# A mixture-of-experts stage whose gate and up products change sides: weight chunks stationary, copied per tile by VectorE

## The chip, the cores and the metric

The kernel runs on one core of a Trainium2 chip. The metric is the device time of one execution in microseconds (us). The kernel before took 1597.97 us, the median of three runs that lie between 1597.82 and 1600.06 us.

## The reference, cut to what matters

The input is 16 x 256 = 4096 rows of 128 numbers. Six blocks follow each other, each on the layer-normalised rows and added back: a quantised feed-forward block, attention, the feed-forward block again, a mixture of experts (MoE), windowed attention, the MoE again. The MoE is the part that the change touches:

```python
logits = xf @ router_w.T                     # 8 experts, top 2 for each row
topk_scores = topk_scores / topk_scores.sum(-1, keepdims=True)
h = jax.nn.silu(xf @ wg) * (xf @ wu)         # per expert: 128 -> 512, twice
acc = acc + w[:, None] * (h @ wd)            # 512 -> 128
```

All of it is float32.

## The kernel before, in words

The rows stay in SBUF as 32 tiles of 128. Each block is a phase; at its end all engines meet (`ended`). In the MoE phase (class `Moe`) the logits and the routing come first. A row goes to two experts, so there are 8192 row copies, sorted by expert and padded to whole tiles of 128 that belong to one expert: `NS = 72` tiles in each of the two MoE phases. The expert of tile n stands in `k.eid`, an integer table in SBUF. After this comes the tile loop, which is what the change touches.

For each tile i:

- GpSimd (POOL) gathers the tile's 128 rows from `rows` in DRAM into slot i % 4 of `k.xs` by an indirect DMA (L1227). After the tile it scatters `k.ys` into `outs` by another (L1236). Its program alternates: gather of tile i+4, once tile i is transposed; scatter of tile i, once `ys` of tile i is written.
- TensorE transposes the gathered rows (`xT`, L982); ScalarE copies the result to `k.xTs` (L1047).
- TensorE makes gate and up (`up`, L990): `xTs`, 128 features by 128 rows, is stationary, and the expert's 512 weight columns of `k.wgu` stream past, at an address that a register gives. Each result has rows on partitions and 512 inner features along the free axis, one PSUM bank each. The bank is 1, 2, 3 or 4, by the tile's parity and by gate or up.
- ScalarE takes silu of gate into `k.sgs` (L1052); VectorE multiplies with up into `k.hs` (L1114, the function `h`).
- TensorE transposes the four 128-column chunks of `hs` into PSUM bank 5 (L1006), ScalarE copies them to `k.hTs` (L1062), and TensorE multiplies the four chunks with the expert's down weights, accumulating in bank 6 (L1016). VectorE copies that to `k.ys` (L1122).

The order of the work is written out by hand, engine by engine; nothing plans it. TensorE's iteration i is: gate of tile i+1, transposes of `hs` of tile i, up of tile i+1, row transpose of tile i+2, down of tile i. It loops over 3 passes of 24 tiles (`UN`). The number of the expert is read from `k.eid` into registers once for each tile (`value_load`, L976). VectorE's iteration i is: `h` of tile i+1, then `ys` of tile i. ScalarE's is: silu of tile i+1, `hTs` of tile i, `xTs` of tile i+2. Each engine waits on counters (semaphores) of the others. `sgs`, `hs` and `hTs` have two slots each, chosen by parity, in a tensor `k.pt` that other phases use too. After the tile loop SP's queue loads the results back and they are weighted and added.

Of the kernel before, what the change touches and what calls it, by code (L numbers as in the profile page):

```python
# [893 lines left out]
class Moe:  # L894
# [4 lines left out]
    def __init__(self, k, name, run, last):  # L899
        self.k, self.run, self.last = k, run, last  # L900
        self.s_xn = k.sem(name + "_xn")
        self.s_xnT_ps = k.sem(name + "_xnT_ps")
        self.s_xnT = k.sem(name + "_xnT")
        self.s_lg_ps = k.sem(name + "_lg_ps")
        self.s_lg = k.sem(name + "_lg")
        self.s_e = k.sem(name + "_e")
        self.s_mask = k.sem(name + "_mask")
        self.s_rank_ps = k.sem(name + "_rank_ps")
        self.s_hot = k.sem(name + "_hot")
        self.s_list_ps = k.sem(name + "_list_ps")  # L910
        self.s_eq = k.sem(name + "_eq")
        self.s_part = k.sem(name + "_part")
        self.s_eid = k.sem(name + "_eid")
        self.s_list = k.sem(name + "_list")
        self.s_xT_ps = k.sem(name + "_xT_ps")
        self.s_xT = k.sem(name + "_xT")
        self.s_gate_ps = k.sem(name + "_gate_ps")
        self.s_silu = k.sem(name + "_silu")
        self.s_up_ps = k.sem(name + "_up_ps")
        self.s_h = k.sem(name + "_h")  # L920
        self.s_hT_ps = k.sem(name + "_hT_ps")
        self.s_hT = k.sem(name + "_hT")
        self.s_y_ps = k.sem(name + "_y_ps")
        self.s_y = k.sem(name + "_y")
        self.s_half = k.sem(name + "_half")
        self.s_added = k.sem(name + "_added")
        self.s_stored = k.sem(name + "_stored")
        self.s_scaled = k.sem(name + "_scaled")

        self.ld0, self.st0 = run * 16 * (NS // RING + 1), run * 16 * (NS // RING)  # L930
        self.ga0 = run * 16 * (NG // RING)
        self.s_ld = [k.sem(f"moe_loaded_{i}") for i in range(RING)]
        self.s_st = [k.sem(f"moe_stored_{i}") for i in range(RING)]
        self.s_ga = [k.sem(f"moe_gathered_{i}") for i in range(RING)]

    def tensor(self, eng):
        k, t = self.k, self.k.nc.tensor

        def transposes(g):
            eng.wait_ge(self.s_xn, g + 1)  # L940
            if g >= 4:
                eng.wait_ge(self.s_xnT, g - 3)
            for j in range(GT):
                last = t.transpose(k.PS[:, g % 4, j * P:(j + 1) * P], k.xng[g][:, j, :], k.ident[:, :])
            last.then_inc(self.s_xnT_ps, 1)

        def logits(g):
            eng.wait_ge(self.s_xnT, g + 1)
            for j in range(GT):
                o = (g * GT + j) * NE  # L950
                last = t.matmul(k.PS[:, 4, o:o + NE], k.xnTg[g % 4][:, j * P:(j + 1) * P], k.rw[:, :],  # L951
                                start=True, stop=True)
            last.then_inc(self.s_lg_ps, 1)
        transposes(0)
        transposes(1)
        for g in range(NG):
            if g + 2 < NG:
                transposes(g + 2)
            logits(g)

        eng.wait_ge(self.s_mask, 1)
        t.matmul(k.PS[:, 5, 0:NT * NE], k.before[:, :], k.chosen[:, :], start=True, stop=True)
        t.matmul(k.PS[:, 6, 0:NT * NE], k.onesb[:, :], k.chosen[:, :], start=True, stop=True).then_inc(self.s_rank_ps, 1)
        for g in range(NG):
            eng.wait_ge(self.s_hot, g + 1)
            eng.wait_ge(self.s_part, g + 1)
            for i in range(2 * GT):
                last = t.matmul(k.PS[:, 7, 0:2 * NL], k.hotb[:, g % 2, i, :], k.hota[:, g % 2, i, :],
                                start=g + i == 0, stop=g == NG - 1 and i == 2 * GT - 1, skip_group_check=True)
            last.then_inc(self.s_list_ps, 1)  # L970
        eng.sem_inc(self.s_hT_ps, CR)
        eng.sem_inc(self.s_y_ps, CR)
        eng.wait_ge(self.s_eid, 1)

        def expert(n):
            return t.value_load(k.eid[0:1, ds(n, 1)], min_val=0, max_val=NE - 1)  # L976

        def xT(n, r, before, back):
            eng.wait_ge(self.s_ld[r], self.ld0 + 16 * before + 16)
            if back:  # L980
                eng.wait_ge(self.s_xT, n - 1)
            t.transpose(k.PS[:, 7 * (r % 2), 0:P], k.xs[:, r, 0:D], k.ident[:, :]).then_inc(self.s_xT_ps, 1)  # L982

        def up(n, p, w, e):
            if w == 0:
                eng.wait_ge(self.s_xT, n + 1)
                eng.wait_ge(self.s_silu, n - 1 + CR)
            else:
                eng.wait_ge(self.s_h, n - 1 + CR)
            t.matmul(k.PS[:, 1 + 2 * p + w, :], k.xTs[:, p, :], k.wgu[:, w, ds(e, 1), :].squeeze(1),  # L990
                     start=True, stop=True).then_inc((self.s_gate_ps, self.s_up_ps)[w], 1)

        xT(0, 0, 0, False)
        xT(1, 1, 0, False)
        e0 = expert(0)
        up(0, 0, 0, e0)
        up(0, 0, 1, e0)
        with eng.Fori(0, NS // UN) as m:
            e1 = expert(UN * m + 1)
            for u in range(UN):  # L1000
                i, p = UN * m + u, u % 2
                up(i + 1, 1 - p, 0, e1)
                eng.wait_ge(self.s_h, i + 1 + CR)
                eng.wait_ge(self.s_hT, i + CR)
                for c in range(FC):
                    last = t.transpose(k.PS[:, 5, c * P:(c + 1) * P], k.hs[:, p, c * P:(c + 1) * P], k.ident[:, :])  # L1006
                last.then_inc(self.s_hT_ps, 1)
                up(i + 1, 1 - p, 1, e1)
                xT(i + 2, (u + 2) % RING, UN // RING * m + (u + 2) // RING, True)
                if u == 0:  # L1010
                    e = expert(i)
                e2 = expert(i + 2) if u + 1 < UN else None
                eng.wait_ge(self.s_hT, i + 1 + CR)
                eng.wait_ge(self.s_y, i + CR)
                for c in range(FC):
                    last = t.matmul(k.PS[:, 6, 0:D], k.hTs[:, p, c * P:(c + 1) * P], k.wdn[:, ds(e, 1), c, :].squeeze(1),  # L1016
                                    start=c == 0, stop=c == FC - 1)
                last.then_inc(self.s_y_ps, 1)
                e, e1 = e1, e2


    def scalar(self, eng):
        k, s = self.k, self.k.nc.scalar
# [14 lines left out]
                                    scale=k.lists[:, P + NL + r:P + NL + r + 1])  # L1038
            last.then_inc(self.s_part, 1)
        eng.sem_inc(self.s_silu, CR)  # L1040
        eng.sem_inc(self.s_hT, CR)

        def xT(n, p, back):
            eng.wait_ge(self.s_xT_ps, n + 1)
# [11 lines left out]
        with eng.Fori(0, NS // RING) as m:  # L1056
            for u in range(RING):
                i, p = RING * m + u, u % 2
                silu(i + 1, 1 - p)
                eng.wait_ge(self.s_hT_ps, i + 1 + CR)  # L1060
                eng.wait_ge(self.s_y_ps, i - 1 + CR)
                s.activation(k.hTs[:, p, :], k.PS[:, 5, :], ACT.Copy).then_inc(self.s_hT, 1)  # L1062
                xT(i + 2, p, True)

        for g in range(NG):
# [8 lines left out]
    def vector(self, eng, ch):  # L1074
# [32 lines left out]
        ch.run(v.tensor_tensor(k.dst[:, :], k.row[:, :], k.lists[:, P:P + NL], ALU.max))  # L1107
        v.tensor_scalar(k.src[:, :], k.dst[:, :], 1, None, ALU.logical_shift_right).then_inc(self.s_list, 1)  # L1108

        def h(n, p):  # L1110
            eng.wait_ge(self.s_silu, n + 1 + CR)
            eng.wait_ge(self.s_up_ps, n + 1)
            eng.wait_ge(self.s_hT_ps, n - 1 + CR)
            v.tensor_tensor(k.hs[:, p, :], k.sgs[:, p, :], k.PS[:, 2 + 2 * p, :], ALU.mult).then_inc(self.s_h, 1)  # L1114
        def tiles(m):
            for u in range(RING):
                i, p = RING * m + u, u % 2
                h(i + 1, 1 - p)
                eng.wait_ge(self.s_y_ps, i + 1 + CR)
                if not isinstance(m, int) or self.run:  # L1120
                    eng.wait_ge(self.s_st[u], self.st0 + 16 * m)
                v.tensor_copy(k.ys[:, u, :], k.PS[:, 6, 0:D]).then_inc(self.s_y, 1)  # L1122
        h(0, 0)
        tiles(0)
        with eng.Fori(1, NS // RING) as m:
# [113 lines left out]
    def sync(self, sp, out):  # L1239
# [5 lines left out]
        for u in range(RING):  # L1245
            sp.wait_ge(self.s_st[u], self.st0 + 16 * (NS // RING))
        sp.wait_ge(self.s_h, NS + 1 + CR)
        def put(g):
            if self.last:
                sp.dma_start(out[g * GT * P:(g + 1) * GT * P, :].rearrange("(t p) d -> p t d", p=P),  # L1250
# [18 lines left out]
class Core:  # L1269


    def __init__(self, nc, ctx):
# [78 lines left out]
        self.xs, self.ys = sb("xs", [P, RING, D]), sb("ys", [P, RING, D])  # L1351
        self.yr = self.pt[:, :, :, :].rearrange("p u a (b r d) -> p u (a b) r d", r=2, d=D)
        self.xTs = sb("xTs", [P, 2, P])
        self.sgs, self.hs, self.hTs = (self.pt[:, i, :, :] for i in range(3))
        self.rows = nc.dram_tensor("rows", ((2 + NT) * P, D), F32, kind="Internal").ap()
        self.outs = nc.dram_tensor("outs", ((2 * NT + RING) * P, D), F32, kind="Internal").ap()
        self.PS = ctx.enter_context(nc.psum_tensor("PS", [P, 8, 512], F32))
# [212 lines left out]
```

## Time and profile before

| | us |
|---|---|
| median of three runs | 1597.97 |
| span of the profiled execution, first to last instruction | 1594.8 |
| TensorE matmuls busy (share of the span) | 1233.0 (77%) |
| TensorE weight loads busy | 799.1 (50%) |
| VectorE busy | 996.9 (63%) |
| ScalarE busy | 714.1 (45%) |
| GpSimd busy | 593.8 (37%) |
| mean granted TensorE clock | 0.885 |

Only the span of the profiled execution is known, not a time of its own that includes what lies around the span. The span is 3.2 us under the median. PE is TensorE's matmuls, PEld its weight loads, DVE is VectorE, ACT ScalarE, POOL GpSimd; PEldq is TensorE's sequencer, which handles register work. In a timeline a line holds the start, the time until the end of the last of its instructions, the engine, the source line, the operation and, in brackets, how long the engine was idle before and what released it. Matmuls overlap: the next one starts before the end of the one in front of it is recorded, so the step from start to start says what one costs in a row.

### The profile page before, as it was taken

Reading aid. Unit: us, or ns where it says so; the run is one execution under the profiler, and the core shown is the slowest. Engines: PE = TensorE matmul, PEld = TensorE weight load, DVE = VectorE, ACT = ScalarE, POOL = GpSimd, SP = SyncE. Lnnn points to the kernel's source line nnn. Section 1 sums busy time; section 2 is a strip of 40 time slices with the busy share of each in tenths; the row PEclk is TensorE's granted clock in tenths of the full one; section 3 lists DMA queues with packets and bytes.
Section 4 is the critical chain, followed back from the end, with each engine's and each line's share of the span. In section 5 each row is a group of like instructions: output and inputs, shape, how many; then the busy total and the mean of one; then the engine's idle time right before and its main releaser. Section 6 shows DMA issues by size and latency. Waiting matters only on the chain.

```text
span 1594.8 us, 31915 instructions
## 1 busy us (share of the span) xinstructions
PE 1233.0 (77%) x10217; PEld 799.1 (50%) x10218; DVE 996.9 (63%) x1974; ACT 714.1 (45%) x1328; POOL 593.8 (37%) x859
## 2 busy tenths in 40 slices
PE   0677479999956776299999915999998728999992
PEld 0355346666634556156666602455554525666661
DVE  5799679999838994822222257889896382223233
ACT  0444225555554442144444451666666323444445
POOL 2122221121101220056565614676775104656561
PEclk9989769999988996589999956999999658999996
DMA  8000034223200001011111133434242101111115
GB/s 254 9 0 0 1 61 63 49 53 60 43 2 1 0 0 53 2 36 42 40 39 40 41 112 67 68 56 79 56 75 34 54 0 32 40 40 41 38 41 171
DMA packets 161956, 75.54 MB, mean 47 GB/s; under 512 B 126539, under 2 KB 153940, under 8 KB 161876
## 3 DMA queue, kind: packets, MB, share of 16 engines
q1 hardware_dynamic: 152404, 55.06, 16.1%
q0 software_dynamic: 9472, 19.42, 4.1%
q8 instruction: 49, 0.80, 0.2%
q14 instruction: 31, 0.25, 0.1%
HBM read 28.69 MB, written 15.86 MB: 28 GB/s over the span
## 4 chain that ended last, share of the span: by engine, by line
PE 54%; DVE 25%; issue 7%; ACT 6%; POOL 3%; DMA 3%; SPq 1%; DVEq 1%; POOLq 0%; ACTq 0%
PE PS L990 16%; PE PS L1016 9%; PE PS L656 4%; PE PS L1006 4%; PE PS L358 2%; DVE sg L790 2%; DVE m L790 2%; PE PS L622 2%; PE PS L638 2%; PE PS L575 2%; PE PS L951 2%; DVE q_amax L266 2%; PE PS L610 1%; ACT pt L1070 1%; SPq L882 1%
## 5 line engine op out<-in xcount | busy, mean ns | idle before, releaser
L990 PE MATMUL PS<-wgu,xTs 128*128 x584 | 303.2, 603 | 4.2 <-issue 3.1
L1114 DVE TENSOR_TENSOR pt<-pt,PS 128x512 f32<-128x512 f32 x146 | 100.5, 688 | 295.4 <-PE PS L990 295.4
L715 ACT ACTIVATE pt<-PS 128x768 f32<-128x768 f32 (+1 forms) x256 | 227.5, 917 | 107.8 <-PE PS L638 56.1
L1227 POOL DMA_INDIRECT xs<-rows,src x152 | 147.8, 972 | 192.9 <-DVE src L1108 147.1
L1236 POOL DMA_INDIRECT outs<-ys,dst x144 | 142.4, 989 | 158.5 <-DVE ys L1122 153.0
L1052 ACT ACTIVATE pt<-PS 128x512 f32<-128x512 f32 x146 | 87.2, 597 | 233.8 <-PE PS L990 233.8
L1016 PEld LDWEIGHTS PS<-wdn,pt 128*128 128x128 f32 x1152 | 139.5, 191 | 55.4 <-issue 55.4
L1016 PE MATMUL PS<-wdn,pt 128*128 x1152 | 162.9, 284 | 0.4 <-issue 0.4
L790 DVE TENSOR_REDUCE m<-PS 128x4 f32<-128x1024 f32 x128 | 149.1, 1218 | 10.5 <-PE PS L575 9.9
L575 PE MATMUL PS<-tables 64*128 64x128 bf16 (+2 forms) x1536 | 131.7, 251 | 0.0
L790 DVE TENSOR_REDUCE sg<-PS 128x6 f32<-128x768 f32 x128 | 117.6, 953 | 20.9 <-PE PS L575 20.0
L358 PE MATMUL PS<-wguT,xqT 128*128 128x352 f32 x256 | 104.2, 560 | 18.3 <-ACT xqT L403 15.0
L1006 PEld LDWEIGHTS PS<-ident,pt 128*128 128x128 f32 x576 | 72.3, 142 | 76.7 <-issue 75.2
L990 PEld LDWEIGHTS PS<-wgu,xTs 128*128 128x128 f32 x584 | 90.1, 194 | 9.6 <-issue 9.6
L312 POOL TENSOR_TENSOR xhq<-q_mg,fscale 128x256 f32<-128x256 f32 (+1 forms) x32 | 31.5, 1004 | 159.4 <-DVE q_mg L288 159.4
L656 PE MATMUL PS<-pt,v 128*32 128x256 f32 (+1 forms) x1408 | 84.6, 358 | 3.7 <-ACT wraw L721 2.7
L863 POOL TENSOR_SCALAR_AFFINE_SELECT pt<-pt 128x256 f32<-128x256 f32 x128 | 54.4, 425 | 87.2 <-ACT pt L715 84.8
L1006 PE MATMUL PS<-ident,pt 128*128 128x128 f32 x576 | 86.7, 273 | 0.0
L342 PE MATMUL PS<-wdT,hqT 128*128 128x128 f32 (+1 forms) x384 | 54.0, 292 | 42.2 <-ACT hqT L418 42.2
L1062 ACT ACTIVATE pt<-PS 128x512 f32<-128x512 f32 x144 | 85.4, 593 | 0.2
L622 PE MATMUL PS<-kT,qT 64*128 64x128 bf16 (+1 forms) x704 | 68.7, 276 | 19.3 <-DMA qT<-qs 6.9
L358 PEld LDWEIGHTS PS<-wguT,xqT 128*128 128x128 f32 x256 | 55.4, 228 | 55.4 <-ACT xqT L403 27.4
(229 smaller groups left out, 2239.5 us busy)
## 6 DMA issues: line engine op xcount, KB each, us to landing
pt<-outs SPq DMA_DIRECT2D x16, 512.0 KB, 5.0
rows<-qT SPq DMA_DIRECT2D x12, 256.0 KB, 2.4
xs<-rows,src POOLq DMA_INDIRECT x152, 2.5
outs<-ys,dst POOLq DMA_INDIRECT x144, 2.3
wgu<-in_L_ffn_w_gate SPq DMA_DIRECT2D x1, 2048.0 KB
wgu<-in_L_ffn_w_up SPq DMA_DIRECT2D x1, 2048.0 KB
wdn<-in_L_ffn_w_down SPq DMA_DIRECT2D x8, 256.0 KB
qT<-hqT SPq DMA_DIRECT2D x128, 4.0 KB
```

The source lines that it names most:

```text
L358: last = t.matmul(k.PS[:, bank + j, 0:I0], k.xqT[:, j * P:(j + 1) * P], k.wguT[:, w, :], start=True, stop=True)
L575: last = t.matmul(cols(k.PS[:, self.bank + u, :]), k.eye2[rows, e, :], table[rows], start=False, stop=e == 1, skip_group_check=True)
L622: t.matmul(k.PS[:, self.bank + u, c:c + n], k.qT[p][rows, a, j * P:(j + 1) * P], k.kT[p][rows, kg, 0:n], start=j == 0, stop=False, skip_gr ...
L656: last = t.matmul(k.PS[32 * u:32 * u + 32, 0, col:col + n], k.v[p][:, kb, g, :], k.pt[:, (2 * a + u // 2) % 4, u % 2, c:c + n], start=kb = ...
L715: s.activation(k.pt[:, a % 4, :, 0:w], k.PS[:, self.bank:self.bank + 2, 0:w], ACT.Exp, scale=self.scale).then_inc(self.s_p, 1)
L790: v.tensor_reduce(out, src, AX.X, ALU.max).then_inc(self.s_nat_read, 1)
L990: t.matmul(k.PS[:, 1 + 2 * p + w, :], k.xTs[:, p, :], k.wgu[:, w, ds(e, 1), :].squeeze(1), start=True, stop=True).then_inc((self.s_gate_ps ...
L1006: last = t.transpose(k.PS[:, 5, c * P:(c + 1) * P], k.hs[:, p, c * P:(c + 1) * P], k.ident[:, :])
L1016: last = t.matmul(k.PS[:, 6, 0:D], k.hTs[:, p, c * P:(c + 1) * P], k.wdn[:, ds(e, 1), c, :].squeeze(1), start=c == 0, stop=c == FC - 1)
L1114: v.tensor_tensor(k.hs[:, p, :], k.sgs[:, p, :], k.PS[:, 2 + 2 * p, :], ALU.mult).then_inc(self.s_h, 1)
L1227: g.indirect_dma_start(k.xs[:, i % RING, :], None, k.rows[:, :], bass.IndirectOffsetOnAxis(ap=k.src[:, i:i + 1], axis=0)).then_inc(self.s_ ...
L1236: g.indirect_dma_start(k.outs, bass.IndirectOffsetOnAxis(ap=k.dst[:, i:i + 1], axis=0), k.ys[:, u, :], None).then_inc(self.s_st[u], 16)
```

## The change

It touches the tile loop of both MoE phases and nothing else.

- A new tile `k.wst` holds, in two slots, the gate and up weights of one tile's expert, 128 partitions by 2 x 512. VectorE fills it for each tile: it reads the expert's number into a register and copies 1024 columns from `k.wgu` (`weights`). In VectorE's iteration this stands between `h` of tile i+1 and `ys` of tile i, and serves tile i+2. Tiles 0 and 1 are copied before the loop.
- Gate and up are now four matmuls each. A chunk of 128 weight columns is stationary and `xTs`, 128 rows wide, moves. The result has 128 inner features on partitions, chunk by chunk, and so the four chunks of `hs` are what down takes as stationary operand.
- The four transposes of `hs`, ScalarE's copy to `hTs`, and `hTs` itself are gone.
- TensorE's iteration i becomes: gate and up of tile i+1, row transpose of tile i+2, read of an expert's number, down of tile i. Gate of tile n waits for the copied weights of tile n as well. The function `h` waits for down of two tiles before, where it waited for the transposes.
- TensorE reads the expert's number once for each tile still, for down.
- SP waits for the last weight copy before it loads into `k.pt`.

```diff
-        self.s_hT_ps = k.sem(name + "_hT_ps")
-        self.s_hT = k.sem(name + "_hT")
+        self.s_wst = k.sem(name + "_wst")
...
-        def up(n, p, w, e):
+        def up(n, p, w):
             if w == 0:
                 eng.wait_ge(self.s_xT, n + 1)
+                eng.wait_ge(self.s_wst, n + 1)
                 eng.wait_ge(self.s_silu, n - 1 + CR)
             else:
                 eng.wait_ge(self.s_h, n - 1 + CR)
-            t.matmul(k.PS[:, 1 + 2 * p + w, :], k.xTs[:, p, :], k.wgu[:, w, ds(e, 1), :].squeeze(1),
-                     start=True, stop=True).then_inc((self.s_gate_ps, self.s_up_ps)[w], 1)
+            for c in range(FC):
+                last = t.matmul(k.PS[:, 1 + 2 * p + w, c * P:(c + 1) * P],
+                                k.wst[:, 1 - p, w, c * P:(c + 1) * P], k.xTs[:, p, :],
+                                start=True, stop=True)
+            last.then_inc((self.s_gate_ps, self.s_up_ps)[w], 1)
...
         with eng.Fori(0, NS // UN) as m:
-            e1 = expert(UN * m + 1)
+            e = expert(UN * m)
             for u in range(UN):
                 i, p = UN * m + u, u % 2
-                up(i + 1, 1 - p, 0, e1)
+                up(i + 1, 1 - p, 0)
+                up(i + 1, 1 - p, 1)
+                xT(i + 2, (u + 2) % RING, UN // RING * m + (u + 2) // RING, True)
+                e1 = expert(i + 1) if u + 1 < UN else None
                 eng.wait_ge(self.s_h, i + 1 + CR)
-                eng.wait_ge(self.s_hT, i + CR)
-                for c in range(FC):
-                    last = t.transpose(k.PS[:, 5, c * P:(c + 1) * P], k.hs[:, p, c * P:(c + 1) * P], k.ident[:, :])
-                last.then_inc(self.s_hT_ps, 1)
-                up(i + 1, 1 - p, 1, e1)
-                xT(i + 2, (u + 2) % RING, UN // RING * m + (u + 2) // RING, True)
-                if u == 0:
-                    e = expert(i)
-                e2 = expert(i + 2) if u + 1 < UN else None
-                eng.wait_ge(self.s_hT, i + 1 + CR)
                 eng.wait_ge(self.s_y, i + CR)
                 for c in range(FC):
-                    last = t.matmul(k.PS[:, 6, 0:D], k.hTs[:, p, c * P:(c + 1) * P], k.wdn[:, ds(e, 1), c, :].squeeze(1),
+                    last = t.matmul(k.PS[:, 6, 0:D], k.hs[:, p, c * P:(c + 1) * P], k.wdn[:, ds(e, 1), c, :].squeeze(1),
                                     start=c == 0, stop=c == FC - 1)
                 last.then_inc(self.s_y_ps, 1)
...
                 silu(i + 1, 1 - p)
-                eng.wait_ge(self.s_hT_ps, i + 1 + CR)
-                eng.wait_ge(self.s_y_ps, i - 1 + CR)
-                s.activation(k.hTs[:, p, :], k.PS[:, 5, :], ACT.Copy).then_inc(self.s_hT, 1)
                 xT(i + 2, p, True)
...
+        def weights(n, p, back):
+            e = v.value_load(k.eid[0:1, ds(n, 1)], min_val=0, max_val=NE - 1)
+            if back:
+                eng.wait_ge(self.s_up_ps, n - 1)
+            v.tensor_copy(k.wst[:, 1 - p, :, :], k.wgu[:, :, ds(e, 1), :].squeeze(2)).then_inc(self.s_wst, 1)
+
         def h(n, p):
             eng.wait_ge(self.s_silu, n + 1 + CR)
             eng.wait_ge(self.s_up_ps, n + 1)
-            eng.wait_ge(self.s_hT_ps, n - 1 + CR)
+            eng.wait_ge(self.s_y_ps, n - 1 + CR)
             v.tensor_tensor(k.hs[:, p, :], k.sgs[:, p, :], k.PS[:, 2 + 2 * p, :], ALU.mult).then_inc(self.s_h, 1)
         def tiles(m):
             for u in range(RING):
                 i, p = RING * m + u, u % 2
                 h(i + 1, 1 - p)
+                weights(i + 2, p, True)
                 eng.wait_ge(self.s_y_ps, i + 1 + CR)
...
+        eng.wait_ge(self.s_eid, 1)
+        weights(0, 0, False)
+        weights(1, 1, False)
         h(0, 0)
...
+        sp.wait_ge(self.s_wst, NS + 2)
...
-        self.sgs, self.hs, self.hTs = (self.pt[:, i, :, :] for i in range(3))
+        self.sgs, self.hs, self.wst = self.pt[:, 0, :, :], self.pt[:, 1, :, :], self.pt[:, 2:4, :, :]
```

## Rows read from the trace of the kernel before

**Rows 1.** Busy time by stretch: feed-forward, first MoE tile loop, second MoE tile loop.

```profile
core 0: us, PE busy (x) PEld busy (x) DVE busy (x) ACT busy (x) POOL busy (x), PEclk, DMA share, GB/s
500.00:600.00 100.00, 74.15 (x364) 51.77 (x362) 92.74 (x146) 44.91 (x86) 24.98 (x25) 0.91 0.00 0
...
680.00:915.00 235.00, 233.26 (x1196) 149.68 (x1197) 69.28 (x141) 97.77 (x212) 136.30 (x140) 0.99 0.13 39
...
1322.00:1556.00 234.00, 230.87 (x1186) 147.90 (x1187) 68.30 (x139) 97.33 (x212) 136.49 (x140) 0.99 0.13 40
```

**Rows 2.** The chain that ended last, one tile: start, us, what.

```profile
802.16 0.97 PE PS L1016 x8
803.13 0.86 PE PS L990 x2
804.00 0.44 PE PS L1006 x4
804.43 0.86 PE PS L990 x2
805.29 0.11 PE PS L982
805.40 1.00 PE PS L1016 x8
```

**Rows 3.** Timeline of one tile in the middle of the first MoE loop.

```profile
801.03 1.02 PE L990 MATMUL PS<-wgu,xTs 128*128 x2
801.29 0.59 ACT L1062 ACTIVATE pt<-PS 128x512 f32<-128x512 f32 x1
801.46 0.14 PEld L982 LDWEIGHTS PS<-ident,xs 128*128 128x128 f32 x1 [0.24 <-issue]
801.80 0.97 POOL L1227 DMA_INDIRECT xs<-rows,src  x1 [0.30 <-issue]
801.89 0.27 PE L982 MATMUL PS<-ident,xs 128*128 128x128 f32 x1
801.98 0.97 PEld L1016 LDWEIGHTS PS<-wdn,pt 128*128 128x128 f32 x8 [0.37 <-issue]
802.01 1.13 PE L1016 MATMUL PS<-wdn,pt 128*128 x8
802.15 0.69 DVE L1114 TENSOR_TENSOR pt<-pt,PS 128x512 f32<-128x512 f32 x1 [1.92 <-PE PS L990]
802.20 0.28 ACT L1047 ACTIVATE xTs<-PS 128x128 f32<-128x128 f32 x1 [0.32 <-PE PS L982]
802.86 0.30 PEld L990 LDWEIGHTS PS<-wgu,xTs 128*128 128x128 f32 x2
802.97 1.02 PE L990 MATMUL PS<-wgu,xTs 128*128 x2
803.17 0.29 DVE L1122 COPY ys<-PS 128x128 f32<-128x128 f32 x1 [0.34 <-PE PS L1016]
803.40 0.14 PEld L1006 LDWEIGHTS PS<-ident,pt 128*128 128x128 f32 x1 [0.24 <-issue]
803.74 0.99 POOL L1236 DMA_INDIRECT outs<-ys,dst  x1 [0.97 <-DVE ys L1122]
803.83 0.60 PE L1006 MATMUL PS<-ident,pt 128*128 128x128 f32 x4
803.84 0.36 PEld L1006 LDWEIGHTS PS<-ident,pt 128*128 128x128 f32 x3 [0.29 <-issue]
804.03 0.60 ACT L1052 ACTIVATE pt<-PS 128x512 f32<-128x512 f32 x1 [1.55 <-PE PS L990]
```

**Rows 4.** Waits of the first MoE loop, 690 to 910 us: total us, times, longest.

```profile
DVE pt L1114 <- PE PS L990: 128.5, 67, 2.9
ACT pt L1052 <- PE PS L990: 107.0, 67, 2.7
POOL outs L1236 <- DVE ys L1122: 65.3, 65, 2.3
```

**Rows 5.** Timeline of the start: one-input VectorE instructions, alone and beside GpSimd.

```profile
22.12 1.33 DVE L109 TENSOR_TENSOR q_xn<-wraw,q_inv 128x1120 f32<-128x1120 f32 x1
23.49 0.74 DVE L116 TENSOR_SCALAR q_mg<-q_xn 128x1120 int32<-128x1120 int32 x1
24.26 0.74 DVE L117 TENSOR_SCALAR q_mg<-q_mg 128x1120 f32<-128x1120 f32 x1
...
26.52 2.54 POOL L142 TENSOR_TENSOR q_mg<-q_xn,q_mg 128x1120 f32<-128x1120 f32 x1 [20.17 <-DVE q_xn L118]
...
26.70 3.12 DVE L1479 CAST tables<-pt 128x1408 bf16<-128x1408 f32 x1
```

**Rows 6.** TensorE's sequencer at L976, 800 to 800.9 us: reading an expert's number.

```profile
L976 PEldq TENSOR_LOAD <-eid x1: 300/300/300, 800.0 to 800.0; - x1
L976 PEldq FUSED_REGOPS  x1: 151/151/151, 800.4 to 800.4; - x1
L976 PEldq SEQ_ASSERT  x1: 18/18/18, 800.6 to 800.6; - x1
```

**Rows 7.** Timeline of TensorE in the feed-forward block, 560 to 580 us.

```profile
559.84 2.63 PE L358 MATMUL PS<-wguT,xqT 128*128 128x352 f32 x8 [0.47 <-ACT xqT L403]
...
564.68 1.60 PE L342 MATMUL PS<-wdT,hqT 128*128 128x128 f32 x12 [1.55 <-ACT hqT L418]
566.45 0.69 PE L350 MATMUL PS<-ident,xhq 128*128 128x128 f32 x2 [0.17 <-POOL xhq L312]
567.69 5.06 PE L358 MATMUL PS<-wguT,xqT 128*128 128x352 f32 x8 [0.55 <-ACT xqT L403]
```

More of the change, by code:

```diff
@@ L970, in tensor @@
             last.then_inc(self.s_list_ps, 1)
-        eng.sem_inc(self.s_hT_ps, CR)
         eng.sem_inc(self.s_y_ps, CR)
@@ L989, in up @@
                 eng.wait_ge(self.s_h, n - 1 + CR)
-            t.matmul(k.PS[:, 1 + 2 * p + w, :], k.xTs[:, p, :], k.wgu[:, w, ds(e, 1), :].squeeze(1),
-                     start=True, stop=True).then_inc((self.s_gate_ps, self.s_up_ps)[w], 1)
+            for c in range(FC):
[3 more added lines that the diff above has]
+            last.then_inc((self.s_gate_ps, self.s_up_ps)[w], 1)
         xT(0, 0, 0, False)
         xT(1, 1, 0, False)
-        e0 = expert(0)
-        up(0, 0, 0, e0)
-        up(0, 0, 1, e0)
+        up(0, 0, 0)
+        up(0, 0, 1)
         with eng.Fori(0, NS // UN) as m:
-            e1 = expert(UN * m + 1)
+            e = expert(UN * m)
             for u in range(UN):
                 i, p = UN * m + u, u % 2
-                up(i + 1, 1 - p, 0, e1)
+                up(i + 1, 1 - p, 0)
+                up(i + 1, 1 - p, 1)
+                xT(i + 2, (u + 2) % RING, UN // RING * m + (u + 2) // RING, True)
+                e1 = expert(i + 1) if u + 1 < UN else None
                 eng.wait_ge(self.s_h, i + 1 + CR)
-                eng.wait_ge(self.s_hT, i + CR)
-                for c in range(FC):
-                    last = t.transpose(k.PS[:, 5, c * P:(c + 1) * P], k.hs[:, p, c * P:(c + 1) * P], k.ident[:, :])
-                last.then_inc(self.s_hT_ps, 1)
-                up(i + 1, 1 - p, 1, e1)
-                xT(i + 2, (u + 2) % RING, UN // RING * m + (u + 2) // RING, True)
-                if u == 0:
-                    e = expert(i)
-                e2 = expert(i + 2) if u + 1 < UN else None
-                eng.wait_ge(self.s_hT, i + 1 + CR)
                 eng.wait_ge(self.s_y, i + CR)
                 for c in range(FC):
-                    last = t.matmul(k.PS[:, 6, 0:D], k.hTs[:, p, c * P:(c + 1) * P], k.wdn[:, ds(e, 1), c, :].squeeze(1),
+                    last = t.matmul(k.PS[:, 6, 0:D], k.hs[:, p, c * P:(c + 1) * P], k.wdn[:, ds(e, 1), c, :].squeeze(1),
                                     start=c == 0, stop=c == FC - 1)
                 last.then_inc(self.s_y_ps, 1)
-                e, e1 = e1, e2
+                e = e1
     def scalar(self, eng):
@@ L1040, in scalar @@
         eng.sem_inc(self.s_silu, CR)
-        eng.sem_inc(self.s_hT, CR)
         def xT(n, p, back):
```

## The prediction

> **What bounds the kernel now.** I read the busy time by stretch first. The change lives in two tile loops of 72 tiles. In both, TensorE is busy 99% of the time at a granted clock of 0.99, while VectorE is busy 29% [rows 1]; 235 us for 72 tiles is 3.26 us each. The chain that ended last says the same in detail: it stays on TensorE all the time, and a tile is 0.97 (down) + 0.86 (gate) + 0.44 (four transposes) + 0.86 (up) + 0.11 (row transpose) = 3.24 us [rows 2]. Then I looked for how close other engines are. The timeline shows ScalarE's `hTs` copy ending at 801.88 and down's first weight load at 801.98, with down's matmul directly behind the row transpose [rows 3]: the handover of `hs` is nearly as long as TensorE's queue. VectorE's long waits are all for TensorE [rows 4]; it has room in total. The question is whether that room is at the right place.
>
> **What TensorE saves.** Gone are four transposes, 0.44 us a tile [rows 2]. Gate and up become four stationary chunks of 128 columns each with 128 moving columns. Down already has exactly that form: eight matmuls for four chunks in 0.97 us [rows 2]. So gate and up cost 0.97 each instead of 0.86, +0.22 together. If TensorE alone set the pace, a tile would be 3.24 - 0.44 + 0.22 = 3.02 us, a gain of 0.22 us. ScalarE loses a copy of 0.59 us [rows 3], which is worth nothing by itself since the engine waits anyway [rows 4].
>
> **What the copy adds.** VectorE's new instruction copies 128x1024 float32 from SBUF to SBUF. No row has it. The nearest are the one-input instructions over 1120 columns, 0.74 us, against 1.33 us for the two-input one of the same width [rows 5]. The first runs at two columns for each cycle in which the second does one. Taking off 96 columns (0.05 and 0.10 us) gives 0.69 us at the fast rate and 1.23 us at the slow one. I take 0.69: it is one-input, float32 and in SBUF, as the 0.74 us rows are; 1.23 is the upper end.
>
> **Where it lies.** VectorE's order is `h` of tile i+1, copy for tile i+2, `ys` of tile i. `h` of tile i+1 waits for up of tile i+1. Gate of tile i+2 waits for the copy for tile i+2. So the copy, although it has two slots and needs nothing but the expert's number, can't start until up of the tile in front is finished, and gate can't start until the copy is finished. That closes a circle over every tile, gate - up - `h` - copy - gate:
>
> - copied weights ready to the first weight load: 0.10, as from the end of `hTs` at 801.88 to down's first load at 801.98 [rows 3].
> - first weight load to the end of the last matmul: down takes 801.98 to 803.14, 1.16 us for four chunks [rows 3]; eight chunks are 1.16 + 0.97 = 2.13.
> - end of up to the start of `h`: 802.05 to 802.15, 0.10 [rows 3]. Silu isn't later: gate ends 0.97 us before up, silu takes 0.60.
> - `h`: 0.69 [rows 3].
> - gap before the copy: VectorE's sequencer reads the expert's number. On TensorE this is 0.30 + 0.15 + 0.02 us and takes from 800.0 to 800.6, while matmuls go on [rows 6]. If VectorE's does it behind the running `h` too, 0.6 us nearly fit under 0.69; addressing and dispatch come on top. Lower end 0, upper end, if it can't overlap at all, 0.75. I take 0.15, near the lower end, as TensorE's row overlaps.
> - copy: 0.69.
>
> The sum is 3.86 us against 3.24: +0.62 us a tile.
>
> What TensorE does meanwhile: after up it has the row transpose and down, 0.11 + 0.97 = 1.08 us, and then waits for some 0.8 us until the weights are there. That wait replaces the saving. Behind it in TensorE's queue stand gate, up, the next row transpose and the next down; none can pass. Everything else fits in the circle: ScalarE's `xTs` (0.28) is ready about 1 us before the weights; `ys` comes right behind the copy, when down has ended already, and is over long before the next `h`. `h`'s new wait for down of two tiles before is met a tile earlier. TensorE's own read of the number stands behind 34 queued instructions and is not seen.
>
> **GpSimd and the copy.** A fast VectorE instruction can collide with GpSimd. The cast of 1408 columns took 3.12 us; at the 0.74 us rows' rate it would be 0.89. It started 0.18 us after a GpSimd instruction of 2.54 us and ended 0.76 us behind it: it stood still until that was over [rows 5]. The same would befall the copy if it met an indirect DMA's preparation. Scatter and gather follow `ys`: 0.04 + 0.29 (`ys`) + 0.28 + 0.99 (scatter) + 0.30 + 0.97 (gather) = 2.87 us after the copy's end [rows 3]. The next copy starts 0.10 + 2.13 + 0.10 + 0.69 + 0.15 = 3.17 us after it. They miss each other by 0.3 us, so I add nothing; and if they touched, copy plus GpSimd's work, 3.56, is shorter than the circle. The Trainium skill's page "SBUF — State Buffer" says of the port pair that VectorE and GpSimd share that the one that comes later "fully blocks", and that a float32 copy in SBUF starves GpSimd of descriptor writes; by that rule the sum would stay 3.86 in this order of events, and grow if the order slips. With the cast row the trace agrees; for indirect DMAs no row shows it.
>
> The two copies ahead of the loop lie in the wait for the first gathered rows; I take 0, at most 1 us a phase if they delay the gathers. SP's new wait is long met. Sum: 144 tiles x 0.62 = +89 us. On the span of 1594.8 that is 1684; with the 3.2 us by which the median exceeds the span, 1687 us. With a gap of 0 it is 3.71 us, +68; with slightly cheaper handovers, +57, 1655.
>
> **The rivals.**
>
> A. **The copy's part is dearer.** At one column per cycle (1.23) the circle is 4.40 us, +167, 1765 us. With the number read in series (0.75) it is 4.46, +176, 1774. For it: no row of a copy with a register address, and none of such a read on VectorE. Against: the 0.74 us rows and the overlapped read on TensorE.
>
> B. **The clock dips.** TensorE gets a regular hole of 0.8 us. In the feed-forward block, with matmuls busy 74%, the clock is 0.91 [rows 1]: after idle gaps of 1.55, 0.17 and 0.55 us the eight matmuls that had taken 2.63 us took 5.06 [rows 7], the lower level of 1.2 GHz. A share of 0.18 at half speed makes 0.91. In that share of tiles the 1.93 us of gate and up double: 0.18 x 144 x 1.9 = 49 us more, 1736 us. Against: busy 3.05 of 3.86 us is 79%, and the hole is short.
>
> C. **Copy and indirect DMAs block each other fully.** If one preparation of 0.97 us stands before each copy, the circle is 4.83 us, +229, 1827 us. It decides from the point where GpSimd's two instructions end over 0.3 us later than I reckon.
>
> D. **The other side: TensorE stays the bound.** This is so if `h`, gap, copy and handovers together take under the 1.08 us of row transpose and down. Then a tile is 3.02, -32 us, 1566 us. Against it stands the order of the code, and `h` and copy alone at 1.38 us. It would need VectorE to do the copy before `h`.
>
> E. **No change:** the circle would have to come to 3.24; with `h` and copy at 1.38 and matmuls at 2.13 it is over that already without any handover.
>
> **How the numbers follow.** My case, 1655 to 1720, gets 0.62; A 0.14; B 0.12; C 0.05; D 0.04; E 0.03. About 0.2%, 3 us, is what a measurement of this kernel can tell from no change. The predicted time is the likeliest case's, 1687. The range takes my case with A and B, 1655 to 1775, and leaves out C, D and E. Slower 0.93, same 0.03, faster 0.04.
>
> **What the profile after would show.** If right: the tile loops last about 278 us instead of 235, the chain of waits goes TensorE, VectorE `h`, VectorE copy, TensorE, once a tile; TensorE's first gate load is released by the copy, after some 0.8 us idle; the copy's row says 0.69 us; down follows the row transpose without a hole; GpSimd's waits for `ys` grow. The copy at 1.2 us or a 0.7 us gap before it means A; a clock near 0.9 means B; copies of uneven length, 1 us and more, mean C; a loop under 3.24 us a tile with TensorE busy throughout would make the circle wrong.

## The result and the profile after

The changed kernel takes 1666.58 us, the median of four runs (1664.79 to 1668.04), beside 1597.91 us for the kernel before: a ratio of 1.042 with an interval of 1.0407 to 1.0433, 69 us slower. The profiled execution took 1668.04 us with a span of 1666.3. The predicted time was 1687 us.

Busy time by stretch shows how the tile loop changed. This is the changed kernel in the middle of its first MoE loop; it answers to [rows 1]:

```profile
core 0: us, PE busy (x) PEld busy (x) DVE busy (x) ACT busy (x) POOL busy (x), PEclk, DMA share, GB/s
700.00:880.00 180.00, 144.39 (x1195) 136.65 (x1194) 75.64 (x144) 41.66 (x96) 93.15 (x96) 1.00 0.12 35
```

TensorE is busy 80% of the time, where it was 99%, at a clock that has not fallen. VectorE has 42%, far from full. So no engine is the bound; a circle of waits must be. How long a tile takes is read from VectorE's copy to `ys`, once for each tile. The rows are of the first MoE loop, the kernel before first, then the changed one; behind the count stand the shortest, median and longest duration in ns, then the start of the first and of the last:

```profile
L1122 DVE COPY ys<-PS x72: 290/292/293, 688.3 to 921.1; 128x128 f32<-128x128 f32 x72
```

```profile
L1118 DVE COPY ys<-PS x72: 271/284/286, 686.5 to 953.8; 128x128 f32<-128x128 f32 x72
```

71 steps in 232.8 us are 3.28 us a tile before, 71 in 267.3 us are 3.76 us after. The difference, 0.49 us, times 144 tiles is 70 us: all of the result.

The timeline of the changed kernel for one tile answers to [rows 3]:

```profile
801.52 0.69 DVE L1109 TENSOR_TENSOR pt<-pt,PS 128x512 f32<-128x512 f32 x1 [2.02 <-ACT pt L1044]
...
802.37 0.69 DVE L1103 COPY pt<-wgu 128x1024 f32 x1 [0.16 <-issue]
802.98 0.28 DVE L1118 COPY ys<-PS 128x128 f32<-128x128 f32 x1
803.13 1.86 PEld L990 LDWEIGHTS PS<-xTs,pt 128*128 128x128 f32 x16 [0.90 <-issue]
803.16 2.02 PE L990 MATMUL PS<-xTs,pt 128*128 128x128 f32 x16 [0.73 <-issue]
803.54 0.99 POOL L1235 DMA_INDIRECT outs<-ys,dst  x1 [1.50 <-DVE ys L1118]
...
804.83 0.97 POOL L1226 DMA_INDIRECT xs<-rows,src  x1 [0.30 <-issue]
804.91 0.14 PEld L980 LDWEIGHTS PS<-ident,xs 128*128 128x128 f32 x1
805.02 0.27 PE L980 MATMUL PS<-ident,xs 128*128 128x128 f32 x1
805.03 0.97 PEld L1010 LDWEIGHTS PS<-wdn,pt 128*128 128x128 f32 x8
805.13 1.06 PE L1010 MATMUL PS<-wdn,pt 128*128 x8
805.23 0.69 DVE L1109 TENSOR_TENSOR pt<-pt,PS 128x512 f32<-128x512 f32 x1 [1.96 <-PE PS L990]
...
806.14 0.69 DVE L1103 COPY pt<-wgu 128x1024 f32 x1 [0.23 <-issue]
...
806.91 1.86 PEld L990 LDWEIGHTS PS<-xTs,pt 128*128 128x128 f32 x16 [0.91 <-issue]
```

(The last of these is gate and up of the next tile.) The circle can be read off: the copy ends at 803.06 and the first weight load starts at 803.13; the sixteenth matmul ends at 805.18 and `h` starts at 805.23; it ends at 805.92, the copy starts at 806.14 and ends at 806.83. That is 0.07 + 2.05 + 0.05 + 0.69 + 0.22 + 0.69 = 3.77 us. In this tile, and in one of four, the step from matmuls to `h` is that short; in the other three `h` starts 0.09 us behind the last matmul and the copy some 0.17 us behind `h`, which comes to the same sum. TensorE has nothing to do for 0.73 us before gate. The profile puts that wait down to "issue"; that the copy releases it has to be read from the times, and is tested below.

### The profile page after: what moved, and what is told of

Its sections match the earlier page's. It is cut to its first block, busy times and chain, and to the rows that moved or that the text cites. A ratio compares the mean times of both kernels' runs of the same rounds, so it can differ in the third digit from the quotient of the medians.

```text
span 1666.3 us, 34422 instructions
## 1 busy us (share of the span) xinstructions
PE 1199.7 (72%) x11393; PEld 913.2 (55%) x11394; DVE 1087.3 (65%) x2123; ACT 642.3 (39%) x1184; POOL 594.5 (36%) x859
## 4 chain that ended last, share of the span: by engine, by line
PE 50%; DVE 24%; issue 12%; ACT 6%; DMA 3%; POOL 3%; SPq 1%; DVEq 1%; ACTq 0%; POOLq 0%
PE PS L990 18%; PE PS L1010 8%; PE PS L656 4%; PE PS L358 2%; PE PS L622 2%; DVE sg L790 2%; DVE m L790 2%; PE PS L638 2%; PE PS L575 2%; DVE q_amax L266 2%; PE PS L950 1%; PE PS L610 1%; ACT pt L1059 1%; DVE q_xn L274 1%; DMA qT<-qs 1%
## 5 line engine op out<-in xcount | busy, mean ns | idle before, releaser
L990 PE MATMUL PS<-xTs,pt 128*128 128x128 f32 x2336 | 297.7, 281 | 104.8 <-issue 104.8
L990 PEld LDWEIGHTS PS<-xTs,pt 128*128 128x128 f32 x2336 | 274.8, 193 | 127.7 <-issue 127.7
L1044 ACT ACTIVATE pt<-PS 128x512 f32<-128x512 f32 x146 | 87.2, 597 | 353.7 <-PE PS L990 353.5
L1010 PE MATMUL PS<-wdn,pt 128*128 x1152 | 152.2, 275 | 0.0
L1103 DVE COPY pt<-wgu 128x1024 f32 x148 | 103.2, 698 | 27.1 <-issue 26.5
L575 PEld LDWEIGHTS PS<-tables 64*128 64x128 bf16 x1536 | 73.2, 98 | 7.8
L342 PEld LDWEIGHTS PS<-wdT,hqT 128*128 128x128 f32 (+1 forms) x384 | 48.9, 204 | 51.9 <-ACT hqT L418 36.1
```

Of the source, the lines that this page charges most:

```text
L342: last = t.matmul(k.PS[:, 7, j * D:(j + 1) * D], k.hqT[0:w, j, c, :], k.wdT[0:w, c, :], start=c == 0, stop=c == 2)
L575: last = t.matmul(cols(k.PS[:, self.bank + u, :]), k.eye2[rows, e, :], table[rows], start=False, stop=e == 1, skip_group_check=True)
L990: last = t.matmul(k.PS[:, 1 + 2 * p + w, c * P:(c + 1) * P], k.wst[:, 1 - p, w, c * P:(c + 1) * P], k.xTs[:, p, :], start=True, stop=True)
L1010: last = t.matmul(k.PS[:, 6, 0:D], k.hs[:, p, c * P:(c + 1) * P], k.wdn[:, ds(e, 1), c, :].squeeze(1), start=c == 0, stop=c == FC - 1)
L1103: v.tensor_copy(k.wst[:, 1 - p, :, :], k.wgu[:, :, ds(e, 1), :].squeeze(2)).then_inc(self.s_wst, 1)
```

## The experiments

The theory is the circle gate - up - `h` - copy - gate, closed by the place of the copy in VectorE's program. The rivals are that the new form of the matmuls costs the time, that the copy's own time or traffic does, or that GpSimd and the copy hold each other up.

**The copy ahead of `h`.**

```diff
-                h(i + 1, 1 - p)
                 weights(i + 2, p, True)
+                h(i + 1, 1 - p)
```

> Only the order on VectorE changes: the copy for tile i+2 stands before h of tile i+1 instead of behind it; no instruction is added or taken away. Theory (the circle gate, up, h, copy, gate sets the pace): the copy leaves the circle, TensorE becomes the bound, a tile takes 2.8 to 3.0 us instead of 3.77, so 1528 to 1566 us, faster than the kernel before (1598). Rival 1 (the form of the matmuls is what costs: 128 columns to each weight load): no change, 1667 us. Rival 2 (the early copy meets GpSimd's scatter, which follows ys, and one of the two stands still): the copy's duration is uneven or the scatter's is longer; where GpSimd's wait gets onto a path that sets the end, 1570 to 1667 us.

Measured: 1527.47 us (1526.2 to 1528.51), ratio to the kernel before 0.9556, interval 0.9536 to 0.9575. Exchanging two lines turns 69 us lost into 71 us gained. Its busy time and timeline:

```profile
core 0: us, PE busy (x) PEld busy (x) DVE busy (x) ACT busy (x) POOL busy (x), PEclk, DMA share, GB/s
700.00:880.00 180.00, 180.00 (x1615) 179.92 (x1614) 108.79 (x194) 56.90 (x130) 133.08 (x129) 1.00 0.16 47
```

```profile
802.06 1.87 PEld L990 LDWEIGHTS PS<-xTs,pt 128*128 128x128 f32 x16
...
802.37 0.29 DVE L1118 COPY ys<-PS 128x128 f32<-128x128 f32 x1 [0.26 <-PE PS L1010]
802.94 1.09 POOL L1235 DMA_INDIRECT outs<-ys,dst  x1 [0.42 <-DVE ys L1118]
803.21 0.69 DVE L1103 COPY pt<-wgu 128x1024 f32 x1 [0.55 <-issue]
...
803.85 0.14 PEld L980 LDWEIGHTS PS<-ident,xs 128*128 128x128 f32 x1
...
803.96 0.97 PEld L1010 LDWEIGHTS PS<-wdn,pt 128*128 128x128 f32 x8
...
804.21 0.69 DVE L1109 TENSOR_TENSOR pt<-pt,PS 128x512 f32<-128x512 f32 x1 [0.30 <-PE PS L990]
...
804.85 1.87 PEld L990 LDWEIGHTS PS<-xTs,pt 128*128 128x128 f32 x16
...
805.73 0.99 POOL L1235 DMA_INDIRECT outs<-ys,dst  x1 [0.43 <-DVE ys L1118]
...
806.37 0.83 DVE L1103 COPY pt<-wgu 128x1024 f32 x1 [0.92 <-issue]
...
807.64 0.53 PEld L990 LDWEIGHTS PS<-xTs,pt 128*128 128x128 f32 x4
```

TensorE is never idle in this stretch. A tile is 804.85 - 802.06 = 2.79 us: gate and up 1.79, row transpose 0.11, down 0.89. The copy ends at 803.90, 0.95 us before the gate that needs it. At the start of each pass of four tiles it comes later (806.37) and takes longer (0.83), and still ends at 807.20, 0.44 us before its gate. The matmul form is not what costs; with it the loop is faster than the old one by 3.28 - 2.79 = 0.49 us a tile.

**No copy in the loop.** The calls of `weights` in the loop, number read and copy, are left out, and gate waits for the first two copies only. So this kernel leaves out work: all tiles after the first two use the weights of tiles 0 and 1.

```diff
-                eng.wait_ge(self.s_wst, n + 1)
+                eng.wait_ge(self.s_wst, 2)
...
-                weights(i + 2, p, True)
...
```

> Leaves out the weight copies and number reads of VectorE in the tile loop (tiles 0 and 1 are still copied, all later tiles use those weights), so gate waits for no copy. Theory (circle): TensorE alone sets the pace, 24 pairs of weight load and matmul at 0.112 to 0.121 us and a row transpose of 0.11 us, 2.8 to 3.0 us a tile: 1528 to 1566 us, and the same as with the copy ahead of h within 5 us. Rival (matmul form): the pace of the loop doesn't change much, 1640 us or more.

Measured: 1526.01 us (two runs, 1523.29 and 1528.72), ratio 0.9544 (0.9513 to 0.9576). The median is within 1.5 us of the run before, and a tile takes 2.79 us in both: ahead of `h`, a copy per tile costs nothing that can be measured.

**The same copy in the kernel before.** Its result goes to a tile that nobody reads.

```diff
...
                 h(i + 1, 1 - p)
+                weights(i + 2)
                 eng.wait_ge(self.s_y_ps, i + 1 + CR)
...
```

> The kernel before, with the same read and copy of 1024 columns put on VectorE behind h of each tile, into a tile that nobody reads. Theory (it is the dependence that costs, not VectorE's time or the traffic): h 0.69, gap, copy 0.69 and ys 0.29 fit into 3.24 us a tile, ys comes up to 0.4 us later and GpSimd with it, and the time stays within 10 us of 1598. Rival (the copy itself costs, by VectorE's time, the memory's ports or GpSimd's blocking): 1620 to 1670 us.

Measured: 1599.86 us, ratio 1.0012 (1.0001 to 1.0023). The instruction that is on the circle in the changed kernel costs 0.1%, at most 0.23%, where nothing waits for it. Most of these copies overlap one of GpSimd's gathers, and they take 0.75 us in the median, more than the 0.69 us in the changed kernel; that costs nothing here either. The cost is the dependence, not VectorE's time.

**The expert's number read ahead of `h`**, with the copy still behind it.

```diff
...
-                h(i + 1, 1 - p)
-                weights(i + 2, p, True)
+                e = read(i + 2)
+                h(i + 1, 1 - p)
+                weights(i + 2, p, True, e)
...
```

> VectorE's sequencer reads the expert's number of tile i+2 before it waits for h of tile i+1, instead of behind h; the copy stays behind h. Theory (circle): the gap of 0.16 to 0.23 us between the end of h and the start of the copy falls to about 0.05, 0.13 us a tile, times 144: 19 us less, 1648 us. Rival (what follows up doesn't set the pace): the same as after, 1667 us.

Measured: 1627.1 us (1625.86 to 1631.35), 40 us below the changed kernel where 19 were expected. The direction is the theory's, the size is double. First what VectorE's sequencer does in the changed kernel, between the start of `h` at 801.52 and the copy at 802.37:

```profile
L1100 DVEq FUSED_REGOPS  x2: 53/122/190, 801.5 to 802.0; - x2
L1100 DVEq TENSOR_LOAD <-eid x1: 301/301/301, 801.6 to 801.6; - x1
L1100 DVEq SEQ_ASSERT  x1: 23/23/23, 802.2 to 802.2; - x1
...
L1103 DVEq FUSED_REGOPS  x1: 57/57/57, 802.3 to 802.3; - x1
```

The read does run while `h` runs, as it does beside matmuls on TensorE [rows 6], but it and the address last 0.16 us beyond `h`'s end at 802.21. With the read first, the timeline of VectorE is:

```profile
802.40 0.69 DVE L1111 TENSOR_TENSOR pt<-pt,PS 128x512 f32<-128x512 f32 x1 [2.02 <-PE PS L990]
...
803.00 0.69 DVE L1105 COPY pt<-wgu 128x1024 f32 x1
803.61 0.28 DVE L1121 COPY ys<-PS 128x128 f32<-128x128 f32 x1
```

The copy starts 0.09 us before the recorded end of `h`. The step from the start of `h` to that of the copy falls from 0.85 to 0.91 us (801.52 to 802.37, 805.23 to 806.14) to 0.60 us, and 0.25 to 0.31 us times 144 tiles is 36 to 45 us, as measured.

**The copy in halves,** behind `h`; gate waits for the first, up for the second.

```diff
-                eng.wait_ge(self.s_wst, n + 1)
+                eng.wait_ge(self.s_wst, 2 * n + 1)
...
+                eng.wait_ge(self.s_wst, 2 * n + 2)
...
-            v.tensor_copy(k.wst[:, 1 - p, :, :], k.wgu[:, :, ds(e, 1), :].squeeze(2)).then_inc(self.s_wst, 1)
+            for w in range(2):
+                v.tensor_copy(k.wst[:, 1 - p, w, :], k.wgu[:, w, ds(e, 1), :].squeeze(1)).then_inc(self.s_wst, 1)
...
```

> The copy stays behind h, but as two of 512 columns each; gate waits for the first, up for the second. Theory (circle): only gate's half lies on the circle, about 0.43 us (0.69 less 256 columns' time at the fast rate, 0.27) instead of 0.69; the second half is done long before up starts. 0.26 us a tile less than the changed kernel, times 144 is 37: 1629 us. A second address computation can cost back some 0.05 us a tile: up to 1637. Rival (VectorE's total time matters): two instructions are dearer than one, 1667 us or more.

Measured: 1627.44 us (1625.14 to 1628.03), as expected. (The expectation's 0.27 us is the time of 512 columns, not of 256.) The copies from 700 to 880 us as a group, and one tile of the timeline:

```profile
L1105 DVE COPY pt<-wgu 128x512 f32 x102 | 38.9, 424 | 10.0 <-issue 10.0
```

```profile
804.09 0.76 DVE L1105 COPY pt<-wgu 128x512 f32 x2 [0.18 <-issue]
804.57 1.86 PEld L991 LDWEIGHTS PS<-xTs,pt 128*128 128x128 f32 x16 [0.63 <-DVE pt L1105]
804.57 2.05 PE L991 MATMUL PS<-xTs,pt 128*128 128x128 f32 x16 [0.44 <-DVE pt L1105]
```

Here the profile itself names the copy as what ends TensorE's wait, while the second half still runs. A half takes 0.42 us instead of 0.69: 0.27 x 144 = 39 us, and 39 us came back. The loop pays one for one for what stands on the circle and nothing for the other half, though VectorE's total rises.

**Read and copy first.** As in the first experiment, with the number read one tile earlier.

```diff
...
-                h(i + 1, 1 - p)
-                weights(i + 2, p, True)
+                weights(i + 2, p, True, e)
+                e = read(i + 3) if u + 1 < RING else None
+                h(i + 1, 1 - p)
...
```

> Copy ahead of h as in the run before, and the expert's number read one tile earlier, so that the copy starts right behind ys, before GpSimd's scatter, which starts 0.28 us after ys. TensorE has no idle time left with the copy ahead of h, so the theory expects the same time, 1527 us within 3. On GpSimd it tells who yields: if a copy and an indirect DMA's preparation exclude each other, the scatter starts late or takes 0.4 us longer, with the copy at an even 0.69; if they only disturb each other, the scatter takes about 0.1 us more than 0.99. Rival (the copy's earlier start still matters): below 1522 us.

Measured: 1528.11 us (1525.95 to 1529.03), no different from 1527.47, as expected. What the run shows of GpSimd stands behind the next experiment.

**The copy on ScalarE.**

```diff
...
+            s.activation(k.wst[:, 1 - p, :, :], k.wgu[:, :, ds(e, 1), :].squeeze(2), ACT.Copy).then_inc(self.s_wst, 1)
...
+                weights(i + 2, p, True)
                 silu(i + 1, 1 - p)
...
```

> The copy is ScalarE's (before silu of tile i+1), VectorE has none. ScalarE's copy of 1024 columns is about 1.02 us by its activation of that width in the attention blocks; with silu 0.60 and xTs 0.28 that is 1.9 us of 2.79, beside TensorE. Theory: no circle contains it, TensorE stays the bound, 1527 us within 5, and GpSimd's scatter is back at 0.99 us and h at 0.69. Rival (ScalarE becomes late: silu or xTs holds up gate through up's wait, with the number's read in the open): 1540 to 1620 us.

Measured: 1528.7 us (1527.75 to 1528.9), no different from 1527.47 either. ScalarE's copy takes 1.06 us and is hidden too. What differs between the last two kernels is GpSimd's scatter. In the stretch from 700 to 880 us, with the copy on ScalarE:

```profile
L1236 POOL DMA_INDIRECT outs<-ys,dst x65 | 64.1, 986 | 34.3 <-DVE ys L1122 30.8 <-issue 3.5
```

and with read and copy first, together with the copy itself:

```profile
L1239 POOL DMA_INDIRECT outs<-ys,dst x65 | 70.9, 1091 | 25.3 <-DVE ys L1122 19.2 <-issue 6.1
...
L1105 DVE COPY pt<-wgu 128x1024 f32 x65 | 46.5, 716 | 14.8 <-issue 14.8
```

With VectorE's copy beside it the scatter takes 0.105 us more on average, and the copy 0.02 us more than its usual 0.694. The averages mix two cases, which the timeline of the run with read and copy first shows:

```profile
777.61 0.68 DVE L1105 COPY pt<-wgu 128x1024 f32 x1
777.97 1.18 POOL L1239 DMA_INDIRECT outs<-ys,dst  x1 [0.57 <-DVE ys L1122]
...
780.30 0.68 DVE L1105 COPY pt<-wgu 128x1024 f32 x1
780.73 1.12 POOL L1239 DMA_INDIRECT outs<-ys,dst  x1 [0.30 <-DVE ys L1122]
```

Where the copy starts first, it keeps its time and the scatter takes 0.13 to 0.19 us more. In every fourth tile the copy starts some 0.64 us after the scatter; then the scatter keeps its 0.99 us and the copy takes 0.83. None of this hits a path that sets the end: in this kernel the copy ahead of `h` on VectorE is as good as one on ScalarE.

## Why the prediction was right, and where its sizes were off

**The circle** was forecast with its terms and the place that closes it. The copy and the gap before it were tested by moving, halving or removing them; the matmuls, `h` and the handovers were only read from the trace. Slower was right, and the median lies in the range. The predicted cost was 89 us, the measured one 69. The difference comes from these terms:

- *First weight load to the end of the last matmul, 2.13.* It measured 2.05. I took down's 0.97 as the price of four more chunks. But down came behind a stall in the kernel before: its first load was held until `hTs` was there. Without the stall down's eight matmuls last 1.06 us (805.13, changed kernel) instead of 1.13 [rows 3]. In a row, a pair of load and matmul steps at 0.112 us: 0.89 us for four chunks, not 0.97.
- *The handovers, 0.10 and 0.10.* They measured 0.07 and, in three tiles of four, 0.09; in the fourth 0.04 to 0.05.
- *The gap before the copy, 0.15.* It measured 0.16 to 0.23, the longer value in the tiles with the shorter handover. The bound of 0 was not the lower one: with the read out of the way the copy starts 0.09 us before the end of `h`.
- *`h` and the copy, 0.69 each.* Both exact; the group of 148 copies has a median of 694 ns. The slow rate (rival A) did not occur, nor did a read in series, though the read is not free either (0.25 to 0.31 us of the circle, by the run with the read first).
- *The base, 3.24 us a tile.* That is a smooth tile; over the loop it was 3.28. It takes 0.04 x 144 = 6 us off the difference, and the members above 0.09 x 144 = 13 or 14.

**TensorE's saving, rival D,** was mis-sized in the same place: 3.02 us a tile was forecast for the case in which TensorE is the bound, 1566 us. With the copy out of the way it is 2.79 us and 1527 us. Gate and up in chunks cost 1.79 us together against 2 x 0.86 [rows 2], only 0.07 more, and down lost its start behind the `hTs` copy. Its condition, that VectorE would do the copy before `h`, was stated rightly; the change does not meet it.

**The clock, rival B,** did not dip: 1.00 from 700 to 880 us with TensorE busy 80% and a hole of 0.73 us in each tile. The feed-forward block with its holes of up to 1.55 us [rows 7] was the wrong neighbour for it; no run shows which property of the holes makes the difference. (The 3.05 us busy that the prediction names under this rival come to 3.02 by its own terms.)

**GpSimd, rival C.** In the changed kernel the gather that ends at 805.80 is followed by a copy at 806.14, so they miss each other by 0.34 us, as reckoned, and 145 of the 148 copies take 0.69 to 0.70 us. So a collision plays no part in the time of this order. One term of the sum had no row behind it, the 0.04 us between the copy's end and `ys`; `ys` starts 0.08 us before that end (802.98 against 803.06), and the error fell on the harmless side. Ahead of the first MoE loop the two copies fall onto the first gather:

```profile
675.22 1.45 DVE L1103 COPY pt<-wgu 128x1024 f32 x2 [0.82 <-issue]
675.30 1.62 POOL L1226 DMA_INDIRECT xs<-rows,src  x1 [72.08 <-DVE src L1097]
```

With the copies on ScalarE that gather takes 1.13 us. So the gather ends 0.5 us later in the first phase, and 0.3 us in the second (1.31 against 1.00), which the sum had bounded at 1.

## What to carry to other kernels

Two buffers do not make a load early: its place in the engine's program does. When work that needs nothing recent is put behind work that waits for the newest result, it inherits that wait; follow producer, consumer and the order on each engine around once per iteration, add up the circle, and compare it with the busiest engine's time per iteration. If every engine has idle time in a steady loop, look for such a circle before looking for a faster instruction; here the cure was to exchange two lines. And take the price of an instruction in a row from a place where it is not the first behind a stall.

## What the runs showed of the hardware that was not expected

- An indirect DMA's preparation on GpSimd and a fast float32 copy on VectorE hold each other up for a part of their time only, and which of the two pays depends on when they meet. A copy that starts 0.27 us into a scatter keeps its 0.69 us, and the scatter takes 1.09 instead of 0.99 (copy ahead of `h`); one that starts 0.64 us into it takes 0.83, and the scatter 0.99; one that starts 0.36 us ahead of it makes the scatter 1.18. In the kernel before with the copy added, the copies meet the gather:

```profile
778.78 0.97 POOL L1237 DMA_INDIRECT xs<-rows,src  x1 [0.30 <-PE PS L983]
...
779.41 0.83 DVE L1114 COPY pt<-wgu 128x1024 f32 x1 [0.16 <-issue]
...
782.00 0.97 POOL L1237 DMA_INDIRECT xs<-rows,src  x1 [0.30 <-PE PS L983]
...
782.59 0.88 DVE L1114 COPY pt<-wgu 128x1024 f32 x1 [0.15 <-issue]
```

  The copies start 0.63 and 0.59 us into the gather and both end 1.46 to 1.47 us after its start, as if each were held until 0.77 us into the gather and then took its 0.69; that it is held so is a reading of the times, not a test. The cast beside GpSimd's two-input instruction had stood still until that ended [rows 5]. The Trainium skill's page "SBUF — State Buffer", section "Who interferes with whom", says of such pairs that the later one "fully blocks" for the whole instruction. That agrees with the cast's row. For indirect DMAs it does not: by that rule (an estimate) the copy that starts 0.59 us into the gather of 0.97 would end 0.97 + 0.69 = 1.66 us after its start, not 1.47, and the one that starts 0.27 us into the scatter would not keep its 0.69. A meeting in the loop costs one of the two 0.1 to 0.2 us.
- A copy whose address stands in a register ran at the fast rate, 0.694 us for 1024 columns.
- Reading a number into a register costs VectorE 0.25 to 0.31 us of a chain even behind a running instruction of 0.69 us, since the next instruction, with nothing to wait for, would otherwise have started before the running one's recorded end.
